# Layer norm row sums and squares on ScalarE instead of VectorE's batch norm passes, with some products moved from GpSimd to VectorE

## The chip, the cores and the metric

The kernel runs on one core of a Trainium2 chip. The metric is the device time of one execution in microseconds (us); lower is better. In a trace PE is TensorE, DVE is VectorE, ACT is ScalarE, POOL is GpSimd and SP is the engine that issues most of the DMAs.

## The reference

The input x has shape (2, 2048, 512). It goes through one block with modulation from a condition vector:

```python
h = layernorm(x) * (1 + ca) + sa
x = x + ga * mamba(h)          # in_proj, causal conv of 4 taps, silu, scan over 16 states, gate, out_proj
h = layernorm(x) * (1 + cb) + sb
x = x + gb * ffn(h)            # sum of 8 factor matrices, / sqrt(8), + bias
```

`layernorm(x)` is `(x - mean) / sqrt(var + 1e-5)` over the 512 features of a row. The heavy part is the scan inside `mamba`: for 1024 channels and 16 states, `s = s * exp(dt*A) + dt*h*B` along the sequence, and then the sum over the states of `s * C`. All data are fp32.

## The kernel before

The two sequences are cut into 16 chunks of 256 rows, taken in turn from the one and the other sequence (`CHUNKS` = 16, `ROWS` = 256, held as `LB` = 2 tiles of 128 rows). A chunk's scan is 64 units, a unit being one state index n for one pair of 128-channel tiles, 2 x 256 elements per partition. `one_round(c, ...)` exists once for each engine and runs 32 steps s of 2 units each; 4 units are a quad, so a chunk has 16 quads g. Every engine has its own fixed instruction order, and semaphores join them.

For each unit ACT computes the decays (two Exp passes, `decays`, L595) into one of three PSUM banks. DVE scans (`scan`, L1264). POOL makes the other scan input four units at a time (`make_ub`, L482, into a ring of `UB_RING` = 3). After the scan the state is multiplied by C, either by DVE (`multiply_c` of the vector block, L1277) or, for the last `POOLED[quad]` units of a quad, by POOL in one instruction for these units (`multiply_c` of the pool block, L520). PE turns the products and sums over n. ACT saves the last column of each state for the next chunk (`keep_carry`, L579), and a decay bank is free for the unit three places further on in the order `FREED` when the scan, or the product, of its unit is done.

Around this scan each round carries the neighbours' work: the first layer norm and projections of chunk c+1 (when `la` is given), and the output projection, the second layer norm and the ffn of chunk c-1 (when `lc` is given).

The statistics of a norm are made like this. DVE runs `bn_stats` on the two row tiles (`stats`, L1284; for the first norm in `stats_before(c + 2)` at s = 31, for the second in `stats_after(c - 1)` at s = 17) and `bn_aggr` (`means`, L1293) at s = 0 and at s = 18. POOL turns the variance into 1/sqrt(var + eps) (`deviations`, L447 and L449, called by `norm_before` at quad 0 and `norm_after` at quad 9, ahead of that quad's `make_ub`). DVE makes the shift, minus mean times that (`shifts`, L1300) at s = 1 and s = 19, between the two scans of the step. ACT normalizes (L602), at s = 3 in `z_before` and at s = 20 in `z_after`. In the second norm the row was finished just before by `residual_mixer` (L1365, L1367) at s = 15 and s = 17.

`scan(unit)` and `scan(unit + 1)` of a DVE step stand with this between them: the product of the unit before, then `means` or `shifts` where the step has them.

Of the kernel before, what the change touches and what calls it, by code (L numbers as in the profile page):

```python
# [22 lines left out]
ALU = mybir.AluOpType  # L23
ACT = mybir.ActivationFunctionType

P = 128
# [15 lines left out]
UB_RING = 3  # L42
# [4 lines left out]
DT_PAIRS = 5  # L47
ON_POOL = (2, 2, 2, 2, 3, 2, 3, 3, 3, 2, 2, 1, 2, 1, 1, 1)
FIRST_POOL = (2, 1, 1, 1, 1, 1, 2, 2, 2, 2, 2, 1, 2, 1, 1, 1)
LAST_POOL = (2, 2, 2, 2, 1, 2, 1, 2, 1, 2, 1, 2, 2, 2, 2, 1)  # L50
POOLED = FIRST_POOL + ON_POOL * (CHUNKS - 2) + LAST_POOL
EARLY = (46, 54)
# [92 lines left out]
def build(nc, x, win_m, xp_t, dt_t, wo_t, chan, cond_t, wmod, factors, bias, out):  # L145
# [9 lines left out]
    with ExitStack() as ctx:  # L155
# [42 lines left out]
        mv_a = sb("mv_a", [P, LB, 2])  # L198
        nrm_a = sb("nrm_a", [P, 2, LB])

        dt = sb("dt", [P, DT_PAIRS, 2, ROWS])
# [18 lines left out]
        mv_c = sb("mv_c", [P, LB, 2])  # L220
        nrm_c = sb("nrm_c", [P, 2, LB])

        mod_row = [hc[0:BATCH, 2 * j:2 * j + 2, :].rearrange("p k r -> p (k r)") for j in range(2)]
# [32 lines left out]

        xc_loaded, bn_c, stats_c, norm_c, z_c = sem("xc_loaded"), sem("bn_c"), sem("stats_c"), sem("norm_c"), sem("z_c")
        tanh_g_made, o_scaled, f_scaled, out_stored = sem("tanh_g_made"), sem("o_scaled"), sem("f_scaled"), sem("out_stored")

# [168 lines left out]
        def _(pool):  # L428
# [13 lines left out]

            def deviations(c, mv, nrm, done, normed, used):

                pool.wait_ge(done, c + 1)
                wait(pool, used, c)
                pool.tensor_tensor(nrm[:, 0, :], mv[:, :, 1], small[:, 1, :], ALU.add).then_inc(normed, 1)  # L447
                pool.wait_ge(normed, NORMS * c + 1)
                pool.tensor_tensor(nrm[:, 0, :], nrm[:, 0, :], small[:, 0, :], ALU.pow).then_inc(normed, 1)  # L449

            def norm_before(c):
                deviations(c, mv_a, nrm_a, stats_a, norm_a, z_a)

            def norm_after(c):
                deviations(c, mv_c, nrm_c, stats_c, norm_c, z_c)

# [78 lines left out]
            def one_round(c, par, la, lc):  # L535
                for g in range(QUADS):
                    quad = QUADS * c + g
                    if la is not None and g == 0:
                        norm_before(c + 1)
                    if lc is not None and g == 9:  # L540
                        norm_after(c - 1)
                    if quad + UB_RING - 1 < QUADS * CHUNKS:
                        make_ub(quad + UB_RING - 1)
                    multiply_c(quad)
                    if g in (0, 2, 3):
                        make_u(c, max(g, 1))
                    if c == 0 and 3 <= g < 3 + RANK - 1:
                        add_factor(g - 2)
                    if la is not None and g == 12:
                        make_u(c + 1, 0)  # L550

            rounds(one_round)
            for t in range(LB):
                pool.wait_ge(stats_c, FINAL + 1 + t)
                if t == 0:
                    pool.wait_ge(z_c, FINAL)
                pool.tensor_tensor(nrm_c[:, 0, t:t + 1], mv_c[:, t, 1:2], small[:, 1, 0:1], ALU.add).then_inc(norm_l, 1)
                pool.wait_ge(norm_l, 2 * t + 1)
                pool.tensor_tensor(nrm_c[:, 0, t:t + 1], nrm_c[:, 0, t:t + 1], small[:, 0, 0:1], ALU.pow).then_inc(norm_l, 1)
# [3 lines left out]
        def _(act):  # L563
# [42 lines left out]
            def modulate(src, dst, j, b, shift, scale):  # L606
# [5 lines left out]
                return last  # L612


            def z_before(c):
# [171 lines left out]
            def one_round(c, par, la, lc):  # L787
                for s in range(STEPS):
# [5 lines left out]
                    if la is not None:  # L794
# [9 lines left out]
                        if s in (23, 27):  # L804
                            soft_dt(c + 1, 2 * (s // 27))
                            soft_dt(c + 1, 2 * (s // 27) + 1)
                    if lc is not None and s == 22:
                        modulate_after(c - 1, 1 - par, 1)
# [20 lines left out]
                    if lc is not None:  # L829
                        if s in (1, 3, 5):  # L830
                            tanh_gate(c - 1, {1: 1, 3: 2, 5: 3}[s])
                        if s == 20:
                            z_after(c - 1)
                        if s == 21:
                            act.wait_ge(mods_made, 4)
                            modulate_after(c - 1, 1 - par, 0)
                    if la is not None and s == 29:
                        tanh_gate(c, 0)
                    if la is None and s in (20, 21, 23, 25):
                        tanh_gate_last({20: 0, 21: 1, 23: 2, 25: 3}[s])  # L840
# [405 lines left out]
        def _(dve):  # L1246
# [48 lines left out]

            def shifts(c, mv, nrm, normed):

                dve.wait_ge(normed, NORMS * c + 2)
                for t in range(LB):
                    dve.tensor_scalar(nrm[:, 1, t:t + 1], mv[:, t, 0:1], nrm[:, 0, t:t + 1], -1.0,  # L1300
                                      ALU.mult, ALU.mult).then_inc(normed, 1)
# [58 lines left out]
            def residual_mixer(c, par, t):  # L1360
# [5 lines left out]
                dve.wait_ge(o_scaled, LB * c + t + 1)  # L1366
                dve.tensor_tensor(xc[:, t, :], bank_c[t][:, :], xc[:, t, :], ALU.add).then_inc(c_free[t], 1)  # L1367

            def stats_after(c):
                dve.wait_ge(c_free[0], C_JOBS * c + 5)  # L1370
                dve.wait_ge(c_free[1], C_JOBS * c + 5)
                stats(c, xc, stat_c, bn_c, stats_c)

# [42 lines left out]
            means(0, stat_a, mv_a, bn_a, stats_a, norm_a)  # L1416
            shifts(0, mv_a, nrm_a, norm_a)
            copy_mod_rows(0)
# [19 lines left out]
            def one_round(c, par, la, lc):  # L1438
                for s in range(STEPS):
# [7 lines left out]
                    if la is not None and s == 0:  # L1447
                        means(c + 1, stat_a, mv_a, bn_a, stats_a, norm_a)
                    if la is not None and s == 1:
                        shifts(c + 1, mv_a, nrm_a, norm_a)  # L1450
                    if lc is not None and s == 18:
                        means(c - 1, stat_c, mv_c, bn_c, stats_c, norm_c)
                    if lc is not None and s == 19:
                        shifts(c - 1, mv_c, nrm_c, norm_c)
                    scan(unit + 1)
# [11 lines left out]
                    if lc is not None:  # L1467
# [6 lines left out]
                        if s in (15, 17):  # L1474
                            residual_mixer(c - 1, 1 - par, s // 17)
                        if s == 17:
                            stats_after(c - 1)
                        if s in (26, 27):
                            scale_ffn(c - 1, 1 - par, s - 26)
                    if la is not None:  # L1480
                        if s == 31 and c + 2 < CHUNKS:
                            stats_before(c + 2)
                        if s in (10, 12, 15, 17):
# [13 lines left out]
            for t in range(LB):  # L1497
# [6 lines left out]
                dve.wait_ge(c_free[t], c_jobs + 1)  # L1504
                if t == 0:
                    dve.wait_ge(stats_c, FINAL)
                dve.bn_stats(stat_c[:, t, :], xc[:, t, :]).then_inc(bn_c, 1)
                dve.wait_ge(bn_c, FINAL + 1 + t)
                if t == 0:
# [37 lines left out]
```

## Time and profile before

| what | value |
|---|---|
| median of 3 runs | 2100.62 us (2098.13 to 2101.44) |
| the profiled execution, its time | 2095.92 us |
| the profiled execution, its span | 2093.7 us |
| busy share of the span: DVE, POOL, PE, ACT | 93%, 91%, 81%, 71% |
| mean granted TensorE clock | 0.958 of full |

The span is the time from the first to the last instruction; 2.2 us of the profiled execution lie outside it. A duration in the trace is that of one instruction from its start to its end. Neighbours on one engine overlap a little, so the time that an instruction takes from its engine is the distance from its start to the start of the next.

### The profile page before, as it was taken

To read this page: it belongs to the slowest core of one execution; us is meant where nothing else is said; L and a number is where in the kernel's file an instruction comes from. 1 tells how busy PE (TensorE), PEld (TensorE's weight loads), DVE (VectorE), ACT (ScalarE), POOL (GpSimd) and SP (SyncE) were. 2 spreads that over 40 slices of the span, in tenths; PEclk is the share of its full clock that TensorE was granted. 3 is DMA by queue.
4 is the path that set the end of the run, shared out by engine and by line. 5 is a ranking of instruction groups with operands and counts; after the bars stand their busy time and mean duration, and the time that the engine had idled before them with its cause. 6 is when DMAs were issued, how large, how long until landed. Compare 5 with 4: busy or idle time off the path is not lost.

```text
span 2093.7 us, 28318 instructions
## 1 busy us (share of the span) xinstructions
PE 1694.9 (81%) x8640; PEld 1236.5 (59%) x8640; DVE 1949.5 (93%) x2473; ACT 1484.6 (71%) x4483; POOL 1905.3 (91%) x936
## 2 busy tenths in 40 slices
PE   7576787888878788888878888787887878788797
PEld 4365656656565665656556575655656565565564
DVE  3688999999999999999999999999999999999995
ACT  3456777687777777777677877767777776877662
POOL 0669999999999999999999999999999999999992
PEclk9778999999999999999999999999999999999998
DMA  6345404123040412304031131413213041310300
GB/s 241 136 101 106 136 21 151 41 92 96 26 151 22 151 41 86 96 32 145 28 136 56 72 106 36 142 31 132 61 52 125 21 152 36 118 60 33 109 26 31
DMA packets 70122, 179.80 MB, mean 86 GB/s; under 512 B 6609, under 2 KB 8273, under 8 KB 61906
## 3 DMA queue, kind: packets, MB, share of 16 engines
q1 hardware_dynamic: 66274, 170.65, 24.1%
q0 software_dynamic: 3696, 7.34, 2.2%
q8 instruction: 69, 1.13, 0.2%
q14 instruction: 83, 0.68, 0.1%
HBM read 169.05 MB, written 8.91 MB: 85 GB/s over the span
## 4 chain that ended last, share of the span: by engine, by line
DVE 49%; issue 19%; ACT 18%; PE 8%; DMA 3%; POOL 2%; DVEq 0%; ACTq 0%; SPq 0%; POOLq 0%
DVE state_p L1264 15%; DVE decay L1264 13%; DVE sc_d L1277 6%; ACT decay L595 6%; DVE bank_a L1317 6%; DMA ffn<-factors 2%; ACT dt L701 2%; DVE hc L1326 2%; ACT L595 2%; ACT L701 2%; DVE yg L1358 2%; PE bank_a L924 1%; PE y_bank L877 1%; DVE yg L1336 1%; POOL ub L482 1%
## 5 line engine op out<-in xcount | busy, mean ns | idle before, releaser
L482 POOL TENSOR_TENSOR ub<-u,b_all 128x2048 f32<-128x2048 f32 x255 | 1160.9, 4553 | 0.0
L595 ACT ACTIVATE decay<-dt,decay_rate 128x256 f32<-128x256 f32 (+1 forms) x2048 | 887.2, 465 | 168.0 <-DVE state_p L1264 165.5
L1264 DVE TENSOR_TENSOR_SCAN decay<-decay,carry,ub 128x512 f32<-128x512 f32 x526 | 656.2, 1273 | 37.3 <-ACT decay L595 16.1
L1264 DVE TENSOR_TENSOR_SCAN state_p<-decay,carry,ub 128x512 f32<-128x512 f32 x498 | 627.0, 1268 | 40.1 <-ACT decay L595 39.1
L520 POOL TENSOR_TENSOR state_p<-state_p,c_all 128x1024 f32<-128x1024 f32 (+2 forms) x256 | 587.9, 2297 | 54.6 <-ACT carry L579 50.6
L877 PE MATMUL y_bank<-ident,sc_d 128*128 128x128 f32 x2104 | 333.7, 290 | 238.5 <-DVE sc_d L1277 238.4
L877 PEld LDWEIGHTS y_bank<-ident,sc_d 128*128 128x128 f32 x2104 | 251.1, 148 | 330.8 <-DVE sc_d L1277 327.0
L1277 DVE TENSOR_TENSOR sc_d<-decay,c_all 128x512 f32<-128x512 f32 x526 | 348.9, 668 | 0.0
L877 PEld LDWEIGHTS y_bank<-ident,state_p 128*128 128x128 f32 x1992 | 236.2, 144 | 114.3 <-POOL state_p L520 71.9
L877 PE MATMUL y_bank<-ident,state_p 128*128 128x128 f32 x1992 | 272.1, 281 | 35.2 <-POOL state_p L520 33.6
L579 ACT ACTIVATE carry<-decay 128x2 f32<-128x2 f32 x526 | 85.6, 163 | 286.4 <-DVE sc_d L1277 286.3
L924 PE MATMUL bank_a<-hT,win_h 128*128 128x256 f32 x992 | 246.2, 393 | 2.3 <-ACT hT L610 2.3
L924 PE MATMUL bank_c<-hT,win_z 128*128 128x256 f32 x960 | 240.8, 399 | 0.0
L1006 PE MATMUL bank_c<-wo,yg 128*128 128x512 f32 x480 | 224.0, 595 | 0.0
L924 PEld LDWEIGHTS bank_c<-hT,win_z 128*128 128x128 f32 x960 | 187.9, 204 | 30.6 <-issue 6.7
L924 PEld LDWEIGHTS bank_a<-hT,win_h 128*128 128x128 f32 x992 | 185.3, 197 | 28.8 <-DVE hc L1326 5.0
L1317 DVE SCALAR_TENSOR_TENSOR bank_a<-pre_z,conv,bank_a 128x256 f32<-128x256 f32 x372 | 150.8, 478 | 11.8 <-ACT bank_a L647 11.8
L1006 PEld LDWEIGHTS bank_c<-wo,yg 128*128 128x128 f32 x480 | 89.1, 191 | 69.2 <-issue 65.6
L1030 PE MATMUL bank_c<-ffn,xa 128*128 128x512 f32 x240 | 123.6, 618 | 0.0
L461 POOL TENSOR_TENSOR u<-dt,hc 128x512 f32<-128x512 f32 x64 | 82.0, 1281 | 41.9 <-ACT dt L701 41.9
L868 PE MATMUL y_bank<-ident,skipped 128*128 128x128 f32 x256 | 41.3, 285 | 89.0 <-ACT y_rows L680 86.8
L680 ACT ACTIVATE y_rows<-y_bank 128x512 f32<-128x512 f32 x64 | 37.7, 589 | 71.6 <-PE y_bank L877 71.6
(135 smaller groups left out, 1765.0 us busy)
## 6 DMA issues: line engine op xcount, KB each, us to landing
win_h<-win_m SPq DMA_DIRECT2D x128, 256.0 KB, 2.6
c_all<-bc_scratch SPq DMA_DIRECT2D x32, 1024.0 KB, 7.4
win_z<-win_m SPq DMA_DIRECT2D x128, 256.0 KB, 2.7
b_all<-bc_scratch SPq DMA_DIRECT2D x31, 1024.0 KB, 4.9
xa<-x SPq DMA_DIRECT2D x16, 512.0 KB, 4.0
xc<-x SPq DMA_DIRECT2D x16, 512.0 KB, 3.7
out<-xc SPq DMA_DIRECT2D x15, 512.0 KB, 6.8
ffn<-factors POOLq DMA_DIRECT2D x7, 1024.0 KB, 9.2
```

The source lines that it names most:

```text
L482: pool.tensor_tensor(ub[:, slot, :, :, :], u[:, (PAIRS * c + q) % U_PAIRS, :, :].unsqueeze(1).to_broadcast([P, QUAD, 2, ROWS]), b_all[:, n ...
L520: pool.tensor_tensor(part, part, c_all[:, n + QUAD - k:n + QUAD, :].unsqueeze(2).to_broadcast([P, k, 2, ROWS]), ALU.mult).then_inc(pooled, 1)
L579: act.activation(dst, src, ACT.Copy).then_inc(carried, 1)
L595: last = act.activation(bk[:, j * ROWS + j:(j + 1) * ROWS], dt[:, pair % DT_PAIRS, j, j:], ACT.Exp, scale=decay_rate[:, e, n:n + 1])
L701: last = act.activation(dt[:, pair % DT_PAIRS, j, :], src, ACT.Softplus, bias=ch[:, e, DT_B:DT_B + 1])
L877: last = pe.matmul(y_bank[:, at:at + P], tile[:, j, t * P:(t + 1) * P], ident[:, :], start=False, stop=last_of_pair, is_transpose=True, sk ...
L924: last = pe.matmul(dst[:, j * ROWS:(j + 1) * ROWS], tile[:, k, :], hTc[:, k, :], start=(k == 0), stop=(k == KD - 1))
L1006: last = pe.matmul(bank_c[t][:, :], yg[:, k, t * P:(t + 1) * P], wo[:, k, :], start=(k == 0), stop=(k == KE - 1))
L1030: last = pe.matmul(bank_c[t][:, :], h2T[:, k, t * P:(t + 1) * P], ffn[:, k, :], start=False, stop=(k == KD - 1))
L1264: dve.tensor_tensor_scan(dst, bk[:, :], ub[:, quad % UB_RING, i, :, :].rearrange("p j r -> p (j r)"), carried_in[:, n, 2 * q:2 * q + 1], A ...
L1277: dve.tensor_tensor(sc_d[:, i % D_RING, :, :], bk[:, :].rearrange("p (j r) -> p j r", j=2), c_all[:, n:n + 1, :].to_broadcast([P, 2, ROWS] ...
L1317: dve.scalar_tensor_tensor(out=part, in0=pre[q % 2][:, j, k:k + ROWS], scalar=conv[:, e, k:k + 1], in1=part, op0=ALU.mult, op1=ALU.add).th ...
```

## The change

ACT takes over the sums. For the first norm of chunk c+2 it runs a Copy pass with an accumulated row sum over each row tile at s = 30 and 31 (`sum_before`), into a PSUM bank whose content nobody reads. DVE turns both sums into minus the mean over sqrt(512) in one `tensor_scalar` of 128x2 (`scaled_means`) at s = 0. ACT then runs two Square passes whose accumulated sum is the variance (`squares_before`) at s = 1. For the second norm the row sum comes out of the residual addition itself, which becomes a `scalar_tensor_tensor` with an accumulated output; DVE scales it at s = 18 (`means_after`) and ACT runs the two Square passes at s = 18 (`squares_after`), between the decays of units 37 and 38. `bn_stats` and `bn_aggr` go, except in the first two chunks' first norm and in the last chunk's second norm. On POOL the deviations of quad 0 and quad 9 move behind that quad's `make_ub`. The shifts of the first norm move from s = 1 to s = 2, those of the second norm move behind the second scan of s = 19. In the 14 middle chunks one product (quad 8) moves from POOL to DVE, and in every second of them (the odd ones) one more (quad 4).

```diff
-ON_POOL = (2, 2, 2, 2, 3, 2, 3, 3, 3, 2, 2, 1, 2, 1, 1, 1)
+ON_POOL = (2, 2, 2, 2, 3, 2, 3, 3, 2, 2, 2, 1, 2, 1, 1, 1)
+ODD_POOL = (2, 2, 2, 2, 2, 2, 3, 3, 2, 2, 2, 1, 2, 1, 1, 1)
-POOLED = FIRST_POOL + ON_POOL * (CHUNKS - 2) + LAST_POOL
+POOLED = FIRST_POOL + (ODD_POOL + ON_POOL) * (CHUNKS // 2 - 1) + LAST_POOL
...
             def norm_before(c):
-                deviations(c, mv_a, nrm_a, stats_a, norm_a, z_a)
+                if c < 2:
+                    pool.wait_ge(stats_a, c + 1)
+                else:
+                    pool.wait_ge(var_a, c - 1)
+                deviations(c, mv_a, nrm_a, norm_a, z_a)
             def norm_after(c):
-                deviations(c, mv_c, nrm_c, stats_c, norm_c, z_c)
+                pool.wait_ge(var_c, c + 1)
+                deviations(c, mv_c, nrm_c, norm_c, z_c)
...
                     quad = QUADS * c + g
+                    if quad + UB_RING - 1 < QUADS * CHUNKS:
+                        make_ub(quad + UB_RING - 1)
                     if la is not None and g == 0:
                         norm_before(c + 1)
                     if lc is not None and g == 9:
                         norm_after(c - 1)
-                    if quad + UB_RING - 1 < QUADS * CHUNKS:
-                        make_ub(quad + UB_RING - 1)
                     multiply_c(quad)
...
+            def sum_before(c, t):
+                if t == 0:
+                    act.wait_ge(xa_loaded, 16 * c + 16)
+                    act.wait_ge(dt_made, PAIRS * c)
+                    wait(act, mean_a, c - 2)
+                act.activation(bank_a[t][:, :], xa[:, t, :], ACT.Copy, accum_out=sum_a[:, t:t + 1]).then_inc(sums_a, 1)
+            def squares(c, src, mv, junk, done):
+                for t in range(LB):
+                    last = act.activation(junk[t][:, :], src[:, t, :], ACT.Square, bias=mv[:, t, 0:1],
+                                          scale=DIM ** -0.5, accum_out=mv[:, t, 1:2])
+                last.then_inc(done, 1)
+            def squares_before(c):
+                act.wait_ge(mean_a, c - 1)
+                squares(c, xa, mv_a, bank_a, var_a)
+            def squares_after(c):
+                act.wait_ge(mean_c, c + 1)
+                squares(c, xc, mv_c, bank_c, var_c)
...
+                    if la is not None and c and s == 1:
+                        squares_before(c + 1)
...
                     decays(2 * step + 1)
...
+                        if s == 18:
+                            squares_after(c - 1)
...
+                    if c + 2 < CHUNKS and s in (30, 31):
+                        sum_before(c + 2, s - 30)
...
+            def scaled_means(c, sums, mv, normed, made):
+                dve.wait_ge(normed, NORMS * c)
+                dve.tensor_scalar(mv[:, :, 0], sums[:, :], -DIM ** -1.5, None, ALU.mult).then_inc(made, 1)
...
-                dve.tensor_tensor(xc[:, t, :], bank_c[t][:, :], xc[:, t, :], ALU.add).then_inc(c_free[t], 1)
-            def stats_after(c):
-                dve.wait_ge(c_free[0], C_JOBS * c + 5)
-                dve.wait_ge(c_free[1], C_JOBS * c + 5)
-                stats(c, xc, stat_c, bn_c, stats_c)
+                if t == 0:
+                    wait(dve, mean_c, c)
+                dve.scalar_tensor_tensor(out=xc[:, t, :], in0=bank_c[t][:, :], scalar=1.0, in1=xc[:, t, :], op0=ALU.mult,
+                                         op1=ALU.add, accum_out=sum_c[:, t:t + 1]).then_inc(c_free[t], 1)
...
                     if la is not None and s == 0:
-                        means(c + 1, stat_a, mv_a, bn_a, stats_a, norm_a)
-                    if la is not None and s == 1:
-                        shifts(c + 1, mv_a, nrm_a, norm_a)
+                        means_before(c + 1)
+                    if la is not None and s == 2:
+                        shifts(c + 1, mv_a, nrm_a, norm_a, DIM ** 0.5 if c else -1.0)
                     if lc is not None and s == 18:
-                        means(c - 1, stat_c, mv_c, bn_c, stats_c, norm_c)
-                    if lc is not None and s == 19:
-                        shifts(c - 1, mv_c, nrm_c, norm_c)
+                        means_after(c - 1)
                     scan(unit + 1)
...
-                        if s == 17:
-                            stats_after(c - 1)
+                        if s == 19:
+                            shifts(c - 1, mv_c, nrm_c, norm_c, DIM ** 0.5)
...
-                        if s == 31 and c + 2 < CHUNKS:
-                            stats_before(c + 2)
```

## Rows read from the trace of the kernel before

**Rows 1.** The page, busy time and share of each engine.
```profile
PE 1694.9 (81%) x8640; PEld 1236.5 (59%) x8640; DVE 1949.5 (93%) x2473; ACT 1484.6 (71%) x4483; POOL 1905.3 (91%) x936
```

**Rows 2.** Tile nrm_a, 200 to 2000 us: durations, first and last start.
```profile
L447 POOL TENSOR_TENSOR nrm_a<-mv_a,small x14: 194/194/197, 225.7 to 1826.4; 128x2 f32<-128x2 f32 x14
```

**Rows 3.** Who waited for whom, 228 to 1829 us, on DVE and POOL: total, times, longest.
```profile
DVE state_p L1264 <- ACT decay L595: 26.9, 28, 1.8
...
POOL nrm_a L447 <- DVE mv_a L1293: 19.8, 13, 1.5
POOL state_p L520 <- ACT carry L579: 9.3, 15, 0.7
```

**Rows 4.** DVE by line and shape: busy us, mean ns, idle before.
```profile
L1277 DVE TENSOR_TENSOR sc_d<-decay,c_all 128x512 f32<-128x512 f32 x526 | 348.9, 668 | 0.0
...
L1300 DVE TENSOR_SCALAR nrm_a<-mv_a,nrm_a 128x1 f32<-128x1 f32 x32 | 5.2, 203 | 4.4 <-POOL nrm_a L449 4.4
...
L1425 DVE TENSOR_SCALAR decay_rate<-decay_rate 128x128 f32<-128x128 f32 x1 | 0.2, 221 | 0.0
L1414 DVE TENSOR_SCALAR conv<-ch 128x40 f32<-128x40 f32 x1 | 0.2, 176 | 0.0
```

**Rows 5.** POOL by line and shape.
```profile
L520 POOL TENSOR_TENSOR state_p<-state_p,c_all 128x1024 f32<-128x1024 f32 x130 | 306.3, 2356 | 12.0 <-ACT carry L579 8.0 <-DVE decay L1264 2.0 <-issue 0.4
L520 POOL TENSOR_TENSOR state_p<-state_p,c_all 128x1536 f32<-128x1536 f32 x56 | 192.5, 3438 | 0.0
```

**Rows 6.** ACT by line and shape.
```profile
L639 ACT ACTIVATE pre_z<-bank_a 128x512 f32<-128x512 f32 x62 | 35.9, 580 | 0.0
...
L602 ACT ACTIVATE xa<-xa,nrm_a 128x512 f32<-128x512 f32 x32 | 24.1, 800 | 5.1 <-DVE nrm_a L1300 5.1
```

**Rows 7.** DVE in order of time around a chunk's start: start, us.
```profile
1084.64 0.66 DVE L1277 TENSOR_TENSOR sc_d<-decay,c_all 128x512 f32<-128x512 f32 x1
1085.22 1.28 DVE L1284 BATCH_NORM_STATS2 stat_a<-xa 128x6 f32<-128x512 f32 x2
1086.41 1.27 DVE L1264 TENSOR_TENSOR_SCAN decay<-decay,carry,ub 128x512 f32<-128x512 f32 x1
1087.60 0.22 DVE L1293 BATCH_NORM_AGGREGATE mv_a<-stat_a 128x2 f32<-128x6 f32 x2
1087.74 1.26 DVE L1264 TENSOR_TENSOR_SCAN decay<-decay,carry,ub 128x512 f32<-128x512 f32 x1
```

**Rows 8.** POOL in order of time around the same chunk's start.
```profile
1085.10 1.28 POOL L520 TENSOR_TENSOR state_p<-state_p,c_all 128x512 f32<-128x512 f32 x1 [0.66 <-ACT carry L579]
...
1088.82 4.53 POOL L482 TENSOR_TENSOR ub<-u,b_all 128x2048 f32<-128x2048 f32 x1
```

**Rows 9.** DVE in order of time, two tensor_scalar operations of 512 elements.
```profile
77.97 4.00 DVE L1404 TENSOR_SCALAR ga<-ga 128x512 f32<-128x512 f32 x1
...
101.87 0.43 DVE L1404 TENSOR_SCALAR gb<-gb 128x512 f32<-128x512 f32 x1
```

**Rows 10.** POOL in order of time, beside the first of these.
```profile
76.75 4.94 POOL L482 TENSOR_TENSOR ub<-u,b_all 128x2048 f32<-128x2048 f32 x1
```

**Rows 11.** DVE in order of time, s = 17 to 19 of the same chunk.
```profile
1155.29 0.69 DVE L1367 TENSOR_TENSOR xc<-bank_c,xc 128x512 f32<-128x512 f32 x1
...
1157.27 0.67 DVE L1326 SCALAR_TENSOR_TENSOR hc<-tanh_s,bank_a 128x512 f32<-128x512 f32 x1
...
1159.05 0.22 DVE L1293 BATCH_NORM_AGGREGATE mv_c<-stat_c 128x2 f32<-128x6 f32 x2
1159.19 1.26 DVE L1264 TENSOR_TENSOR_SCAN decay<-decay,carry,ub 128x512 f32<-128x512 f32 x1
...
1160.95 1.27 DVE L1264 TENSOR_TENSOR_SCAN state_p<-decay,carry,ub 128x512 f32<-128x512 f32 x1
```

**Rows 12.** POOL in order of time, quad 8 of the same chunk.
```profile
1157.58 3.43 POOL L520 TENSOR_TENSOR state_p<-state_p,c_all 128x1536 f32<-128x1536 f32 x1
```

**Rows 13.** ACT in order of time, after the decays of unit 38.
```profile
1161.07 0.17 ACT L579 ACTIVATE carry<-decay 128x2 f32<-128x2 f32 x1 [3.27 <-DVE sc_d L1277]
```

More of the change, by code:

```diff
@@ L199, in build @@
         nrm_a = sb("nrm_a", [P, 2, LB])
+        sum_a = sb("sum_a", [P, LB])
         dt = sb("dt", [P, DT_PAIRS, 2, ROWS])
@@ L221, in build @@
         nrm_c = sb("nrm_c", [P, 2, LB])
+        sum_c = sb("sum_c", [P, LB])
         mod_row = [hc[0:BATCH, 2 * j:2 * j + 2, :].rearrange("p k r -> p (k r)") for j in range(2)]
@@ L257, in build @@
         xc_loaded, bn_c, stats_c, norm_c, z_c = sem("xc_loaded"), sem("bn_c"), sem("stats_c"), sem("norm_c"), sem("z_c")
+        sums_a, mean_a, var_a, mean_c, var_c = sem("sums_a"), sem("mean_a"), sem("var_a"), sem("mean_c"), sem("var_c")
         tanh_g_made, o_scaled, f_scaled, out_stored = sem("tanh_g_made"), sem("o_scaled"), sem("f_scaled"), sem("out_stored")
@@ L441, in _, with deviations @@
             pool.wait_ge(ident_set, 2)
-            def deviations(c, mv, nrm, done, normed, used):
-                pool.wait_ge(done, c + 1)
+            def deviations(c, mv, nrm, normed, used):
                 wait(pool, used, c)
@@ L553, in _ @@
             for t in range(LB):
-                pool.wait_ge(stats_c, FINAL + 1 + t)
+                pool.wait_ge(stats_c, 1 + t)
                 if t == 0:
@@ L1294, in means, with means_before, means_after, shifts @@
                 last.then_inc(done, 1)
-            def shifts(c, mv, nrm, normed):
+            def scaled_means(c, sums, mv, normed, made):
+                dve.wait_ge(normed, NORMS * c)
+                dve.tensor_scalar(mv[:, :, 0], sums[:, :], -DIM ** -1.5, None, ALU.mult).then_inc(made, 1)
+            def means_before(c):
+                if c < 2:
+                    means(c, stat_a, mv_a, bn_a, stats_a, norm_a)
+                else:
+                    dve.wait_ge(sums_a, LB * (c - 1))
+                    scaled_means(c, sum_a, mv_a, norm_a, mean_a)
+            def means_after(c):
+                for t in range(LB):
+                    dve.wait_ge(c_free[t], C_JOBS * c + 5)
+                if c:
+                    scaled_means(c, sum_c, mv_c, norm_c, mean_c)
+                else:
+                    dve.tensor_scalar(mv_c[:, :, 0], sum_c[:, :], -DIM ** -1.5, None, ALU.mult).then_inc(mean_c, 1)
+            def shifts(c, mv, nrm, normed, factor):
                 dve.wait_ge(normed, NORMS * c + 2)
                 for t in range(LB):
-                    dve.tensor_scalar(nrm[:, 1, t:t + 1], mv[:, t, 0:1], nrm[:, 0, t:t + 1], -1.0,
+                    dve.tensor_scalar(nrm[:, 1, t:t + 1], mv[:, t, 0:1], nrm[:, 0, t:t + 1], factor,
                                       ALU.mult, ALU.mult).then_inc(normed, 1)
@@ L1416, in _ @@
             means(0, stat_a, mv_a, bn_a, stats_a, norm_a)
-            shifts(0, mv_a, nrm_a, norm_a)
+            shifts(0, mv_a, nrm_a, norm_a, -1.0)
             copy_mod_rows(0)
@@ L1504, in _ @@
                 dve.wait_ge(c_free[t], c_jobs + 1)
-                if t == 0:
-                    dve.wait_ge(stats_c, FINAL)
                 dve.bn_stats(stat_c[:, t, :], xc[:, t, :]).then_inc(bn_c, 1)
-                dve.wait_ge(bn_c, FINAL + 1 + t)
+                dve.wait_ge(bn_c, 1 + t)
                 if t == 0:
```

## The prediction

> **What bounds the kernel now.** I read the busy shares of the page first. DVE and POOL are both over 90% busy, ACT has 29% of the span free [rows 1]. The norm of one chunk comes 123.1 us after that of the last: 14 of them lie from 225.7 to 1826.4 us, 13 distances [rows 2]. So the 14 middle chunks carry 1,723 us of the span, and each microsecond per chunk is worth about 14. The waits over 13 of these chunks are few [rows 3]. DVE waits 26.9 us for decays of ACT (its largest wait), 2.1 per chunk. POOL waits in two places only: 19.8 us for DVE's mean (1.52 at each chunk's start) and 9.3 us for a carry at quad 15. So both engines stand close to the limit, DVE a little closer, and whatever stops either of them in mid-chunk is paid nearly in full.
>
> **What DVE loses and gains.** An instruction's price is the distance between starts. Two `bn_stats` take 1.19 us, from 1085.22 to 1086.41, and two `bn_aggr` take 0.14 us, from 1087.60 to 1087.74 [rows 7]. A chunk has two of each pair: 2.66 us go. Added are 21 products over 14 chunks, 1.5 per chunk, at 0.58 us (1084.64 to 1085.22 [rows 7]), which is 0.87 us. The two `tensor_scalar` of 128x2 are not in the trace. They lie between a `bn_aggr`'s distance of 0.07 and the 0.20 of the 128x1 form [rows 4]; I take 0.1 each. The accumulated output of the two additions isn't in the trace either. It costs from nothing to another small instruction, 0.2; I take 0.1 each. That is 1.27 us added, so DVE is shorter by 1.39 us per chunk (1.1 to 1.6), 19.5 us over 14 chunks.
>
> **What POOL gains.** One product is 3438 - 2356 = 1,082 ns of a POOL instruction [rows 5], so 1.6 us per chunk, and its 1.52 us of waiting for the mean has work in front of it now. POOL is the looser of the two afterwards, so this covers DVE's gain and adds nothing to it.
>
> **What ACT gets.** Six passes of 128x512 per chunk, between 580 ns (no pointer operand) and 800 ns (two) [rows 6]. I take 0.65 us of ACT's time each and 0.1 for the accumulated sum (0 to 0.2), so 4.5 us, plus 1.5 more carries and seams. ACT is free for 29% of 123 us, some 35 us, so the amount is covered. The Copy passes at s = 30 and 31 fall where it waits for DVE. The place of one pair is not covered. `squares_after` stands between the decays of units 37 and 38 and waits for `mean_c`, which DVE makes at s = 18 just before scan 37. From there DVE has 1.76 us of work until scan 38 (1159.19 to 1160.95 [rows 11]). ACT needs about 0.1 to start, 1.5 for two squares, and 0.1 and 0.87 for carry and decays: 2.6 us. Before, these decays were long made, since ACT then sat 3.27 us [rows 13]. So DVE waits 0.8 us at each second norm (0.3 to 1.2 with the bounds of the passes), 12 us over 15 chunks. At s = 1 the same pair stands before the decays of unit 3, which need DVE's product of unit 0 anyway, so it is hidden. If Square needed a function table of its own, there would be four loads more per chunk on ACT; I expect none.
>
> **The new step that matters: two elements on DVE while POOL works.** The trace shows what a `tensor_scalar` with an immediate, from SBUF to SBUF, does beside POOL [rows 9, 10]. One of 512 elements takes 0.43 us in one case and 4.00 us in another. In the long case it began at 77.97, POOL's product had run since 76.75 and ended at 81.69, and the DVE operation ended at 81.97. It stood still until POOL's instruction was over. Undisturbed it needs 0.43 us for elements for which `tensor_tensor` needs 0.67 [rows 4], so it runs at a doubled rate. Small ones do too: from 40 to 128 elements the time grows by 45 ns, 0.51 ns per element [rows 4]. The 128x1 form shows no such stop, its mean is 203 ns though POOL was at work beside nearly all of them [rows 4]. The new form with two elements lies between them. I hold it for one that stops, since it is the doubled form with one element for each half.
>
> The Trainium skill (VectorE: DVE Perf Modes, Mode 2×_2P) states that this mode needs one source and the destination in SBUF and an even outermost dimension. By that two elements run in it and one doesn't; no row here shows a two-element form. By the row of the 128x1 form the sum below would be 2093 us, by the rule it stays as it is.
>
> Where do the two land? Take the second norm first. `means_after` came at 1159.05 [rows 11]. In the new order DVE is there earlier by 1.24 us (one `bn_stats` pair, `bn_aggr` less the new one) and by 1.28 (the 1.98 us from 1155.29 to 1157.27 become 0.7), and later by 0.1 (the first accumulated output) and 0.58 (the moved product of quad 8): 1157.2, and 1157.8 in odd chunks, which move one more. POOL's product of quad 8 began at 1157.58 [rows 12]. POOL starts its chunk's first `make_ub` at 1086.34 in place of 1088.82 [rows 8] and does the 0.9 us of the norm behind it, so it is 1.6 us earlier: 1156.0, until 1158.3 with two units. In even chunks DVE waits 1.1 us for it. In odd chunks POOL is 1.08 us earlier still: it ended at 1157.3, and the next `make_ub` of 4.55 us has begun, to 1161.8. DVE waits 4.0 us. Seven of each are 35.7 us (0 to 4.6 each is the bound).
>
> At the chunk's start it is a near tie. Without `bn_stats` scan 0 starts at 1085.22, and the new operation is due 1.19 us on, at 1086.41 [rows 7]. POOL's product of quad 15 ends at 1085.10 + 1.28 = 1086.38, and `make_ub` follows it at once now, since the norm no longer stands in front of it [rows 8]. If POOL is first, DVE stops for 4.53 us, less some hundredths; if DVE is first, for nothing. The starts speak for POOL by 0.07 us. But a POOL instruction needs some time from its start to its first read, and in the one case at hand DVE got in between two of POOL's instructions [rows 9, 10]. I take DVE as first, at a little better than even.
>
> **The sum.** -19.5 + 12 + 35.7 = +28.2 us. The deviations behind `make_ub` at quad 9 come 0 to 1 us late for DVE's shifts of s = 19, in chunks where DVE has not just waited; I take nothing, since the wait for ACT covers it. Against its own time the profiled execution goes from 2095.92 to 2124.1. The median of the runs is 4.7 us above the profiled one, so 2129 us.
>
> **Rivals.**
> 1. POOL is first at the chunk's start, in most chunks. The Trainium skill (SBUF — State Buffer, Who interferes with whom) says that whoever issues first holds the shared pair for its whole instruction; the trace agrees, 3.7 us of waiting in [rows 9, 10]. The price: 14 x 4.45 = 62 us more, less what DVE then finds done: 2129 + 60 = 2189 us. Half of the chunks give 2160. For it speaks the order of the starts, against it that 0.03 us of a shorter scan decides. Chance 0.28.
> 2. The small operation does not stop, as the 128x1 form doesn't. Only the gain, the wait for the squares and a late shift remain: -19.5 + 12 + 0 to 5 us, 2093 to 2098. Chance 0.14.
> 3. The clean gain, the other side: nothing stops DVE, and the squares are done in time because ACT's passes cost the lower bound. It decides when two squares with their sums take under 0.8 us or the decays of unit 38 are still done in time: -19.5 (to -22) us, 2081 us (2078 to 2085). For it speaks ACT's 3.27 us of rest at this place [rows 13], against it the order of ACT's instructions. Chance 0.22.
>
> **Chances and range.** The forecast (stops at s = 18, none or few at s = 0) has 0.36; its own range is 2108 to 2150, from the bounds of the passes and of the 35.7 us. Within 0.2% (4.2 us, about what runs of this kernel can tell) falls the upper part of rival 2. Faster: 0.22 and part of 0.14, together 0.28. Same: 0.08. Slower: 0.36 + 0.28, 0.64. The range must take in rivals 1 and 3 to leave out no more than 2 in 10: 2077 to 2188.
>
> **What would show each step.** The idle time of POOL before L447 is gone. The new `tensor_scalar` is short (0.1 to 0.2 us) where POOL is idle or between instructions, and 1 to 4.6 us long where POOL works; its longest ends stand just behind the end of a POOL instruction. DVE waits for the decays of unit 38 by 0.8 us at each second norm. The distance of chunks is 123.1 + 2 = 125 us; at 127 or more rival 1 holds, at 121.7 rival 3. The prediction is wrong if the two-element form doesn't take the second port, if POOL's phase at quad 8 is another than worked out (half a microsecond there moves 4.5 us per chunk), or if the tie goes to POOL.

## The result

The changed kernel takes 2202.74 us (median of 4 runs, 2200.18 to 2203.27) against 2099.38 us for the kernel before: 1.049 times its time, 95% interval 1.047 to 1.051. The forecast was 2129 us with a range to 2188 us. The direction was right and the size was not: 103 us came, 28 were forecast, and the time lies above the range.

### The profile page after: what moved, and what is told of

The parts are those of the page before. It is cut to its first block and busy times, and to the rows that moved or that the text cites. A ratio compares the mean times of both kernels' runs of the same rounds, so it can differ in the third digit from the quotient of the medians.

```text
span 2200.9 us, 28516 instructions
## 1 busy us (share of the span) xinstructions
PE 1735.6 (79%) x8640; PEld 1275.7 (58%) x8640; DVE 1983.8 (90%) x2437; ACT 1551.1 (70%) x4697; POOL 1884.2 (86%) x936
## 5 line engine op out<-in xcount | busy, mean ns | idle before, releaser
L603 ACT ACTIVATE decay<-dt,decay_rate 128x256 f32<-128x256 f32 (+1 forms) x2048 | 887.0, 465 | 130.5 <-DVE state_p L1301 128.2
L528 POOL TENSOR_TENSOR state_p<-state_p,c_all 128x1024 f32<-128x1024 f32 (+2 forms) x256 | 565.4, 2209 | 183.5 <-ACT carry L587 183.0
L1301 DVE TENSOR_TENSOR_SCAN decay<-decay,carry,ub 128x512 f32<-128x512 f32 x547 | 682.7, 1275 | 38.4 <-ACT decay L603 16.3
L1301 DVE TENSOR_TENSOR_SCAN state_p<-decay,carry,ub 128x512 f32<-128x512 f32 x477 | 602.8, 1270 | 47.6 <-ACT decay L603 46.4
L914 PE MATMUL y_bank<-ident,sc_d 128*128 128x128 f32 x2188 | 353.9, 297 | 207.7 <-DVE sc_d L1314 207.3
L914 PEld LDWEIGHTS y_bank<-ident,sc_d 128*128 128x128 f32 x2188 | 273.4, 153 | 296.6 <-DVE sc_d L1314 290.4
L1314 DVE TENSOR_TENSOR sc_d<-decay,c_all 128x512 f32<-128x512 f32 x547 | 363.2, 668 | 0.0
L914 PE MATMUL y_bank<-ident,state_p 128*128 128x128 f32 x1908 | 267.2, 284 | 33.2 <-POOL state_p L528 31.9
L961 PE MATMUL bank_c<-hT,win_z 128*128 128x256 f32 x960 | 248.3, 408 | 0.0
L905 PE MATMUL y_bank<-ident,skipped 128*128 128x128 f32 x256 | 47.4, 316 | 135.9 <-ACT y_rows L711 133.8
L905 PEld LDWEIGHTS y_bank<-ident,skipped 128*128 128x128 f32 x256 | 31.4, 159 | 150.1 <-issue 147.2
```

What stands on the lines that cost most here:

```text
L528: pool.tensor_tensor(part, part, c_all[:, n + QUAD - k:n + QUAD, :].unsqueeze(2).to_broadcast([P, k, 2, ROWS]), ALU.mult).then_inc(pooled, 1)
L603: last = act.activation(bk[:, j * ROWS + j:(j + 1) * ROWS], dt[:, pair % DT_PAIRS, j, j:], ACT.Exp, scale=decay_rate[:, e, n:n + 1])
L914: last = pe.matmul(y_bank[:, at:at + P], tile[:, j, t * P:(t + 1) * P], ident[:, :], start=False, stop=last_of_pair, is_transpose=True, sk ...
L961: last = pe.matmul(dst[:, j * ROWS:(j + 1) * ROWS], tile[:, k, :], hTc[:, k, :], start=(k == 0), stop=(k == KD - 1))
L1301: dve.tensor_tensor_scan(dst, bk[:, :], ub[:, quad % UB_RING, i, :, :].rearrange("p j r -> p (j r)"), carried_in[:, n, 2 * q:2 * q + 1], A ...
L1314: dve.tensor_tensor(sc_d[:, i % D_RING, :, :], bk[:, :].rearrange("p (j r) -> p j r", j=2), c_all[:, n:n + 1, :].to_broadcast([P, 2, ROWS] ...
```

## The profile after

The span is 2200.9 us. Its busy shares, in the order of the page:

```profile
PE 1735.6 (79%) x8640; PEld 1275.7 (58%) x8640; DVE 1983.8 (90%) x2437; ACT 1551.1 (70%) x4697; POOL 1884.2 (86%) x936
```

Both bounding engines lost share against [rows 1]: 3 points on DVE, 5 on POOL. DVE's busy time even grew, by 34 us, though it has fewer passes. So part of its busy time is standing still, and POOL now waits. The norm's place in each chunk (tile nrm_a, 200 to 2000 us, durations and first and last start):

```profile
L450 POOL TENSOR_TENSOR nrm_a<-mv_a,small x14: 196/196/198, 232.0 to 1928.0; 128x2 f32<-128x2 f32 x14
```

That is 130.5 us per chunk in place of 123.1 [rows 2]. DVE's two new operations, tiles mv_a and mv_c (durations minimum, median, maximum in ns):

```profile
L1336 DVE TENSOR_SCALAR mv_a<-sum_a x14: 708/4466/4497, 225.1 to 1921.9; 128x2 f32<-128x2 f32 x14
...
L1336 DVE TENSOR_SCALAR mv_c<-sum_c x14: 156/158/1408, 428.1 to 2114.8; 128x2 f32<-128x2 f32 x14
```

The same operation on 128x2 takes 4.47 us at the chunk's start and 0.16 us at s = 18. The waits from 228 to 1829 us, the stretch of [rows 3], which holds 12 of these longer chunks (total us, times, longest), DVE and then POOL:

```profile
DVE nrm_c L1357 <- POOL nrm_c L452: 52.6, 12, 4.6
DVE state_p L1301 <- ACT decay L603: 30.2, 24, 1.8
...
POOL state_p L528 <- ACT carry L587: 121.8, 65, 4.0
POOL nrm_a L450 <- ACT bank_a L634: 16.4, 12, 1.4
```

The first line is new: 4.4 us each time for the deviation of the second norm. POOL waits 121.8 us for carries in place of 9.3 [rows 3]: in part because it is ahead while DVE stands, in part, 2.6 to 4.0 us per chunk, at quad 8 for the reason told below. The 16.4 us before the first norm's deviation were 19.8 us before the change; they are now a wait for the squares.

In order of time, the start of one chunk, DVE and then POOL (start, us). It answers to [rows 7, 8]:

```profile
1136.51 1.28 DVE L1301 TENSOR_TENSOR_SCAN decay<-decay,carry,ub 128x512 f32<-128x512 f32 x1
1137.70 4.46 DVE L1336 TENSOR_SCALAR mv_a<-sum_a 128x2 f32<-128x2 f32 x1
1142.08 1.28 DVE L1301 TENSOR_TENSOR_SCAN decay<-decay,carry,ub 128x512 f32<-128x512 f32 x1
```

```profile
1136.39 1.28 POOL L528 TENSOR_TENSOR state_p<-state_p,c_all 128x512 f32<-128x512 f32 x1 [0.67 <-ACT carry L587]
1137.62 4.52 POOL L490 TENSOR_TENSOR ub<-u,b_all 128x2048 f32<-128x2048 f32 x1
```

`make_ub` began 0.08 us ahead of the operation, ended at 1142.14, and the operation ended at 1142.16. DVE lost 1142.08 - 1137.70 = 4.38 us, less the 0.1 that the operation needs by itself. Here are steps 17 to 19 of the chunk before, on DVE, POOL and ACT. They answer to [rows 11 to 13]:

```profile
1078.04 1.27 DVE L1301 TENSOR_TENSOR_SCAN state_p<-decay,carry,ub 128x512 f32<-128x512 f32 x1
...
1082.35 0.16 DVE L1336 TENSOR_SCALAR mv_c<-sum_c 128x2 f32<-128x2 f32 x1
...
1084.95 1.28 DVE L1301 TENSOR_TENSOR_SCAN state_p<-decay,carry,ub 128x512 f32<-128x512 f32 x1 [0.69 <-ACT decay L603]
...
1092.37 0.33 DVE L1357 TENSOR_SCALAR nrm_c<-mv_c,nrm_c 128x1 f32<-128x1 f32 x2 [4.36 <-POOL nrm_c L452]
```

```profile
1084.30 2.35 POOL L528 TENSOR_TENSOR state_p<-state_p,c_all 128x1024 f32<-128x1024 f32 x1 [3.94 <-ACT carry L587]
1086.62 4.52 POOL L490 TENSOR_TENSOR ub<-u,b_all 128x2048 f32<-128x2048 f32 x1
...
1091.64 0.69 POOL L452 TENSOR_TENSOR nrm_c<-nrm_c,small 128x2 f32<-128x2 f32 x1
```

```profile
1082.54 0.69 ACT L634 ACTIVATE bank_c<-xc,mv_c 128x512 f32<-128x512 f32 x1 [1.38 <-DVE mv_c L1336]
...
1083.87 0.19 ACT L634 ACTIVATION_READ_ACCUMULATOR bank_c<-xc,mv_c 128x1 f32 x1
1083.97 0.19 ACT L587 ACTIVATE carry<-state_p 128x4 f32<-128x4 f32 x1
```

Read them from the bottom up. The carry of POOL's units of quad 8 could be taken when their last scan ended (1079.31), but in ACT's order it stands behind the squares, and these wait for DVE's mean (1082.35 plus its 0.16). So POOL's product starts at 1084.30, after 3.94 us of waiting. `make_ub` begins at 1086.62, and the deviation stands behind it until 1092.33. DVE wanted it at 1088.0.

Per chunk this is 4.38 - 0.1 at the start, 4.36 at step 19, and 0.5 more of waiting for decays (0.69 at unit 38, where DVE had not waited before, less 0.17 that it had waited for them some units later), less the forecast gain of 1.4: 7.7 us. Measured are 130.5 - 123.1 = 7.4 as a mean over 13 distances. Over the whole span, DVE by line and shape (busy us, mean ns, idle before):

```profile
L1336 DVE TENSOR_SCALAR mv_a<-sum_a 128x2 f32<-128x2 f32 x14 | 58.9, 4204 | 0.0
...
L1357 DVE TENSOR_SCALAR nrm_c<-mv_c,nrm_c 128x1 f32<-128x1 f32 x30 | 5.0, 209 | 62.9 <-POOL nrm_c L452 62.9
...
L1426 DVE DVE_READ_ACCUMULATOR xc<-bank_c,xc 128x1 f32 x30 | 2.5, 83 | 0.0
```

## The experiments

Lines are cut to their core. Each kernel is the changed one with the edit named, unless said otherwise. Ratios are to the kernel before, run on the same chip; its median was 2096.28 us beside the first four experiments, 2096.75 and 2099.9 us beside later ones, so kernels measured on different chips are compared by their distance from it. The changed kernel was 103 us above it.

**Each two-element operation as two of one element.**

```diff
-dve.tensor_scalar(mv[:, :, 0], sums[:, :], -DIM ** -1.5, None, ALU.mult).then_inc(made, 1)
+for t in range(LB):
+    last = dve.tensor_scalar(mv[:, t, 0:1], sums[:, t:t + 1], -DIM ** -1.5, None, ALU.mult)
+last.then_inc(made, 1)
```

> The changed kernel with each 128x2 tensor_scalar of the scaled means split into two of 128x1, nothing else. Theory (the two-element form takes the port that POOL holds, the one-element form doesn't): the 14 stops of 4.4 us at the chunk's start go, and the wait for the second norm's deviation stays at 4.3 us per chunk, since POOL still waits there for a carry behind the squares: 14 x 4.4 = 61 us less, 2141 us. Rival (the operation really waits for something else at that point, ScalarE's sums or the semaphores): the first of the two takes 4 us and more, and the time stays at 2203 us. Second rival (POOL's lead over DVE comes from the stop, and without it the second wait shrinks too): 2085 to 2120 us.

Measured: 2145.96 us, 1.024 (1.022 to 1.025), 50 us above the kernel before. Its operations and its largest wait:

```profile
L1337 DVE TENSOR_SCALAR mv_a<-sum_a x28: 142/147/152, 222.8 to 1867.7; 128x1 f32<-128x1 f32 x28
...
DVE nrm_c L1361 <- POOL nrm_c L452: 56.8, 13, 4.5
```

In order of time at one chunk's start, POOL and then DVE:

```profile
1109.21 4.54 POOL L490 TENSOR_TENSOR ub<-u,b_all 128x2048 f32<-128x2048 f32 x1
...
1109.28 0.19 DVE L1337 TENSOR_SCALAR mv_a<-sum_a 128x1 f32<-128x1 f32 x2
```

All 28 take 0.15 us at the place where one of two elements took 4.47, and `make_ub` has begun 0.07 us ahead of them as it had there. The data and the place are the same, so it is the form: two elements stop beside a working POOL, one doesn't. (The two lie a step of two apart in `mv_a`; a dense pair wasn't tried, but the dense 512 elements of [rows 9] stopped too.) The wait at step 19 is untouched, so it has a cause of its own and doesn't hang on the stop.

**The second norm's deviation in front of `make_ub` at quad 9 again**, as it stood before the change.

```diff
+                    if lc is not None and g == 9:
+                        norm_after(c - 1)
                     if quad + UB_RING - 1 < QUADS * CHUNKS:
                         make_ub(quad + UB_RING - 1)
...
-                    if lc is not None and g == 9:
-                        norm_after(c - 1)
```

> The changed kernel with norm_after of quad 9 back in front of that quad's make_ub on POOL, nothing else. Theory (DVE's shifts of step 19 wait because the deviation stands behind a make_ub of 4.5 us that begins late): the deviation is done 0.4 us before DVE wants it, the wait of 4.3 us goes, 14 x 4.4 = 61 us less, 2141 us; the stop of 4.4 us at the chunk's start stays. Rival (the wait comes from ScalarE's squares being late, whatever POOL's order): the wait stays over 3 us, 2190 us or more. Second rival (the make_ub that is now 0.9 us later makes DVE wait for its scan input): 2150 us or more, with waits of DVE for ub.

Measured: 2099.22 us, 1.001 (1.000 to 1.002). Nearly all of the loss was gone: 3 us above the kernel before in place of 103, so 100 us where the theory said 61. The wait at step 19 went as expected, though POOL still waits 3.96 us for the late carry at quad 8 (2.6 to 4.0 us in each chunk):

```profile
1036.87 2.35 POOL L528 TENSOR_TENSOR state_p<-state_p,c_all 128x1024 f32<-128x1024 f32 x1 [3.96 <-ACT carry L587]
...
1040.50 0.31 DVE L1357 TENSOR_SCALAR nrm_c<-mv_c,nrm_c 128x1 f32<-128x1 f32 x2
```

That the stop at the chunk's start shrank too, from 4.47 to 0.43 us with the two-element form in place, was in no expectation:

```profile
L1336 DVE TENSOR_SCALAR mv_a<-sum_a x14: 409/428/667, 224.9 to 1823.8; 128x2 f32<-128x2 f32 x14
```

Its POOL, at one chunk's start; the two-element operation ran from 1086.48, for 0.42 us:

```profile
1085.61 1.27 POOL L528 TENSOR_TENSOR state_p<-state_p,c_all 128x512 f32<-128x512 f32 x1
1086.84 4.53 POOL L490 TENSOR_TENSOR ub<-u,b_all 128x2048 f32<-128x2048 f32 x1
```

In the changed kernel this product of quad 15 had waited 0.67 us for its carry, and in the kernel before 0.66 us [rows 8]. A POOL that waits there is released by DVE's own progress, and its `make_ub` then begins 0.06 to 0.08 us ahead of DVE's operation. It is so at every chunk's start with this wait, in every kernel traced here that has the operation at this place. Now there is no such wait. DVE no longer gives POOL 4.4 us in mid-chunk, so POOL reaches quad 15 later, DVE's operation comes 0.4 us before that product ends, and goes in between. So the stop at the chunk's start hung on the wait at step 19: a wait of DVE puts POOL ahead, and a POOL that is ahead has just begun a `make_ub` when DVE's operation comes. The reverse doesn't hold, as the run with one-element operations showed.

**Both edits.**

> Both edits: two 128x1 operations in place of each 128x2 one, and the second norm's deviation in front of make_ub. Theory (two separate stops that add): 2203 - 61 - 61 = 2081 us, so under the kernel before (2099 us) by 0.9%. Rival (the two stops cover one work of POOL's, and taking both away shows POOL as the bound): 2100 us or more.

Measured: 2100.76 us, 1.002 (1.001 to 1.003), where the theory said 2081. The two gains don't add, since moving the deviation already takes most of the stop with it. The trace has one more thing. DVE waits 1.9 to 3.6 us for decays in four chunks, three early and one late, 10.9 us in all, behind an ACT that waits 4.03 us for TensorE in the first of them. TensorE's matmuls took twice as long just before, and the granted clock was near half (us, then busy time and number of PE, PEld, DVE, ACT, POOL, granted clock, DMA):

```profile
437.00:443.00 6.00, 6.00 (x19) 3.24 (x18) 4.19 (x5) 4.65 (x14) 5.97 (x2) 0.58 0.00 1
443.00:452.00 9.00, 8.22 (x42) 5.20 (x39) 5.42 (x7) 4.77 (x15) 7.11 (x5) 1.00 0.32 117
```

Of 2.4 GHz this is near the lower level of 1.2, after TensorE had waited 1.95 us for a product of POOL's at 431.5. In the other two early chunks it was 0.56 and 0.57, in the late one 0.66, and 1.00 in seven chunks without such a wait. Why it fell in these four wasn't tried. They bear out the coupling: at the chunk's start that follows each of the four, `make_ub` begins 0.08 us ahead of DVE's operation, and in the middle chunks without such a wait POOL is still in its product of quad 15 there.

**The operation of the first norm in front of scan 0**, 1.2 us earlier.

```diff
+                    if la is not None and s == 0 and c:
+                        means_before(c + 1)
                     scan(unit)
...
-                    if la is not None and s == 0:
+                    if la is not None and s == 0 and not c:
                         means_before(c + 1)
```

> The changed kernel with the 128x2 operation of the first norm in front of scan 0 of its chunk instead of behind it, so that it arrives 1.2 us earlier. Theory (it stops until whichever POOL instruction runs at its arrival is over): it now meets POOL's product of quad 15 (1.28 us) and is done just behind its end, 1.2 to 1.4 us after its start instead of 4.5: 14 x 3.1 = 43 us less, 2160 us. Rival (the stop always lasts for a make_ub, because POOL's next instruction gets in first): 4.5 us and more as before, 2203 us or more. Rival (it waits for ScalarE's sum): it would end at the same moment as before the edit, 2203 us.

Measured: 2157.27 us, 1.029 (1.027 to 1.031), 61 us above the kernel before in place of 103: 42 us less, where the first theory said 43. The operation:

```profile
L1336 DVE TENSOR_SCALAR mv_a<-sum_a x14: 1177/1182/1509, 223.0 to 1879.5; 128x2 f32<-128x2 f32 x14
```

The stop lasts for the rest of the POOL instruction that is running, here the 1.28 us product. POOL's next one doesn't get in first. With the wait at step 19 in place (52.6 us, as in the changed kernel) this edit saves only the stop.

**The squares of the second norm behind the decays of unit 38.**

```diff
-                        if s == 18:
-                            squares_after(c - 1)
...
+                    if lc is not None and s == 19:
+                        squares_after(c - 1)
                     decays(2 * step + 1)
```

> The changed kernel with the squares of the second norm one place later on ScalarE, behind the decays of unit 38, nothing else. Theory (POOL's product of quad 8 starts 4 us late because the carry of unit 35 stands in ScalarE's order behind the squares, which wait for DVE's mean; the late make_ub then holds the deviation and DVE's shifts): that product starts at once, DVE's wait of 4.4 us for the deviation shrinks to about 1.1 us, and its wait of 0.7 us for the decays of unit 38 goes; the stop at the chunk's start may stay: 14 x 4.0 = 56 us less, 2147 us; if the stop goes too, as it did when the deviation was moved, 2090 us. Rival (only the place of the deviation behind make_ub matters): the wait stays over 4 us, 2190 us or more.

Measured: 2163.86 us, 1.032 (1.031 to 1.034), 67 us above the kernel before: 36 us less than the changed kernel, not 56. The carry is free and POOL's product starts early, but the two-element operation of s = 18 then meets it:

```profile
L1336 DVE TENSOR_SCALAR mv_c<-sum_c x14: 816/1466/1569, 425.0 to 2079.7; 128x2 f32<-128x2 f32 x14
...
DVE nrm_c L1357 <- POOL nrm_c L452: 11.6, 12, 1.2
```

Per chunk 4.36 + 0.69 us went and 1.38 + 0.97 came, 2.7 us, 38 us in all. The stop at the chunk's start stayed at 4.46 us. This is the stop at s = 18 that the prediction had described; in the changed kernel the late carry had kept POOL away from it.

**The same with one-element operations.**

> The changed kernel with one-element scaled means and the squares behind the decays of unit 38; the deviation stays behind make_ub. Theory (with the squares moved, what DVE loses at steps 18 and 19 is one make_ub that ends too late, 1.4 us of it at the two-element operation and 1.0 us at the shifts, and without the two-element form all 2.3 us stand at the shifts; at the chunk's start 4.4 us go): 2164 - 14 x 4.4 = 2103 us, with 2 to 2.5 us of waiting for the deviation in each chunk. Rival (the 1.4 us were DVE's own and go as well): 2083 us.

Measured: 2110.01 us, 1.005 (1.003 to 1.006), 7 us over the first theory's time. The wait at the shifts over 13 chunks:

```profile
DVE nrm_c L1361 <- POOL nrm_c L452: 29.6, 13, 2.5
```

That is 2.3 us each: the 1.4 us moved there, as the theory said. What sets DVE's time past this place is the end of one `make_ub`; without the stop DVE only comes to it earlier and waits longer. It also parts the 4.36 us of the changed kernel: 2.3 us come from the deviation's place behind `make_ub` alone, the other 2 from the late carry.

**Three edits: one-element operations, deviation first, squares later.**

> Three edits: one-element scaled means, deviation of the second norm in front of make_ub, squares behind the decays of unit 38. Theory (what was left over the arithmetic gain was 0.7 us per chunk of DVE waiting for decays behind the squares, 0.3 us of the two-element operation and 0.5 us near step 27): 122.3 us per chunk go to 121.7, some 10 us under the kernel with the first two edits, 2088 us, 0.4% under the kernel before. Rival (DVE then catches up with ScalarE at the table loads of steps 23 and 27 and waits there): 2097 us, no gain over the kernel before.

Measured: 2074.85 us, 0.989 (0.988 to 0.991). Better than the theory by 13 us; the theory started from the kernel with two edits, whose four long waits for decays (10.9 us, at the lower clock) are gone here. 121.6 us per chunk are left. This kernel has the whole change without its stops and late shifts, and is 22 us faster than the kernel before.

**The three edits and the products as before the change.**

```diff
-ON_POOL = (2, 2, 2, 2, 3, 2, 3, 3, 2, 2, 2, 1, 2, 1, 1, 1)
+ON_POOL = (2, 2, 2, 2, 3, 2, 3, 3, 3, 2, 2, 1, 2, 1, 1, 1)
-POOLED = FIRST_POOL + (ODD_POOL + ON_POOL) * (CHUNKS // 2 - 1) + LAST_POOL
+POOLED = FIRST_POOL + ON_POOL * (CHUNKS - 2) + LAST_POOL
```

> The same three edits and the products as in the kernel before (1.5 per chunk back from DVE to POOL). Theory (DVE is the bound, at 0.58 us per product): 0.9 us per chunk less, 12 us under the kernel with the three edits, 2076 us. Rival (POOL, at 1.08 us per product, is the bound once DVE has lost its norm passes): 2088 to 2110 us, with DVE waiting for ub.

Measured: 2061.42 us, 0.983 (0.982 to 0.984), the fastest of all. Its chunk takes 120.6 us, and POOL's waits are down to this over 13 chunks:

```profile
POOL state_p L528 <- ACT carry L587: 1.2, 1, 1.2
POOL state_p L528 <- issue: 0.4, 2, 0.2
```

**The kernel before with the new split of the products alone.**

> The kernel before with the new split of the products alone, statistics untouched. Theory (DVE bound): 21 products x 0.58 us = +12 us, 2108 us, 0.6% slower. Rival (POOL bound before): up to 10 us faster. Rival (balanced, each has slack for it): within 4 us of the kernel before.

Measured: 2110.02 us, 1.006 (1.005 to 1.008), 13 us slower. Together with the run before (13 us between the two splits) this prices the moved products: DVE pays for them in either kernel, and what POOL is spared doesn't shorten the time.

**The fastest kernel with the two-element operations back.**

> The fastest kernel so far (2061 us: one-element scaled means, deviation in front of make_ub, squares behind the decays of unit 38, products as in the kernel before) with the two-element operations put back, all else kept. Theory (the form stops for the rest of whatever POOL runs): in that kernel's trace the operation at the chunk's start falls 0.4 us before the end of POOL's product of quad 15, which costs 0.3 us per chunk, 4 us in all; the one at step 18 falls 0.07 us behind the start of POOL's product of quad 8 of 3.4 us, which may cost up to 3.4 us per chunk more: between 2065 and 2112 us, the largest stops ending just behind an end of POOL's. Rival (the form is harmless once the other two places are mended): 2061 us.

Measured: 2160.49 us, 1.028 (1.027 to 1.030), 61 us above the kernel before where the same kernel with one-element operations was 35 below it, and 48 us over the upper end of the theory:

```profile
L1336 DVE TENSOR_SCALAR mv_a<-sum_a x14: 421/4496/4503, 225.4 to 1887.6; 128x2 f32<-128x2 f32 x14
...
L1336 DVE TENSOR_SCALAR mv_c<-sum_c x14: 1390/3120/3354, 417.9 to 2079.0; 128x2 f32<-128x2 f32 x14
```

The theory read the phases off a trace without stops, and had the one at s = 18 right (3.1 us in the median). That stop puts POOL ahead, and the next chunk's start then costs 4.5 us. The order of events shows it: the operation at 347.5 us took 0.42 us, the first long stop at s = 18 came at 417.9, and every chunk's start from 473.6 us on stopped for 4.5. It is the same one-way coupling, set off this time by the operation itself.

## Why the prediction was wrong

- **What bounds the kernel**: right. DVE bounds it more than POOL; 21 products cost 13.3 us, 0.63 us each where 0.58 were taken. (POOL had three places where it waited, not two: 1.8 us for DVE's scans was left out, which changes nothing.)
- **What DVE loses and gains**: right in size. The kernel with the three edits is 21.9 us faster than the one before, where this term said 19.5. ACT's squares were right too: 0.72 us each with the read of the sum (0.69 us and its 0.19 overlap a little), 0.75 taken. The accumulated output of DVE is an instruction of 0.083 us that the next one overlaps wholly: 0.62 us from the addition's start to the next, where another `scalar_tensor_tensor` of this size takes 0.59 or 0.60 (0.1 was taken), the 128x2 form undisturbed takes 0.16 us and 0.05 of distance.
- **Two elements on DVE while POOL works**: right. By the rule of the Trainium skill (VectorE: DVE Perf Modes, Mode 2×_2P) both ports are used when source and destination lie in SBUF and the outermost dimension that isn't one is even, or odd and equal in both. The prediction left out the odd case, without effect here: two elements meet the rule, one leaves no such dimension. The runs agree, 4.47 us against 0.15 at the same place.
- **The near tie at the chunk's start**: wrong side. POOL was first by 0.08 us, which is the 0.07 that was read from the starts, and it was set aside for an argument about its first read. This is rival 1, with 13 stops of 4.4 us. The prediction's argument left out what decides it: where POOL waits for the carry of quad 15, it is just ahead each time, and where it doesn't, DVE comes while the product still runs and stops for 0.43 us.
- **The stop at s = 18, 35.7 us forecast**: wrong step. The phase of POOL was worked out from its own chain alone. That its product of quad 8 waits for a carry that stands behind the squares in ACT's order was not followed, though these squares were seen to wait for DVE's mean. POOL came 2.6 to 4.0 us later than its own work asked, so DVE's operation met nothing (0.16 us). With the squares moved away the stop was there, 1.47 us in every chunk.
- **The deviation behind `make_ub`, "0 to 1 us late", taken as nothing**: the term of the sum that failed most. It was 4.36 us per chunk, 63 us in all. About half of it is the late carry, the rest the place behind `make_ub`: with an early carry 2.3 us stayed, and with the deviation in front all of it went, late carry or not. The reason given for nothing, that the wait for ACT covers it, failed too: DVE waited 0.69 us for the decays of unit 38 (0.8 were forecast), and still 4.36 us for the deviation.
- **The sum**: 19.5 us of gain stand against 57 us of the tie (58.9 less 14 x 0.16), 63 of the deviation and 7 for the decays of unit 38 (0.5 per chunk): +107.5 us, and the two spans differ by 107.2 (the medians by 103). That it closes so well is partly luck, since the gain in it is the forecast one. The range ended 1 us short of rival 1's own 2189 us and had no case with both.

What the terms don't show is that they were coupled in one direction, from a wait in mid-chunk to the stop at the next chunk's start; the run with the deviation moved back showed it, and the last run confirmed it. Left open: why TensorE's clock fell in four chunks of one kernel.

## What to carry to other kernels

When an instruction that waits is put into an engine's order, go through everything behind it until the next instruction that the engine would have waited for anyway, the few-element copies too: a carry of 0.19 us behind two squares and a deviation of 0.9 us behind a `make_ub` led to 63 us of waiting here. On DVE beside a busy POOL, give a small `tensor_scalar` one element per partition, or accept that its price is whatever POOL has left of its instruction. And where two engines run neck and neck, a wait of one shifts where the other is when they next meet, so price stops together, not one by one.

## What the runs showed of the hardware

- A `tensor_scalar` of 128x2 from SBUF to SBUF takes 0.16 us alone and up to 4.5 us beside a POOL `tensor_tensor`, ending 0.02 or 0.03 us behind that one's end; those of 128x1 take 0.14 to 0.16 us each, with POOL in a product, in a `make_ub` or idle.
- With starts 0.08 us apart the earlier one went first: 13 of the 14 operations at a chunk's start stopped for 4.4 us or more. A DVE operation that already waits when a POOL instruction ends goes ahead of POOL's next one, which costs that one nothing that can be seen: in the kernel with the deviation moved back these `make_ub` took 4.53 us, the others 4.54.
- Square with a bias operand and an accumulated sum, 128x512 from SBUF to PSUM: 0.68 us and 0.19 us for the read of the sum; two of them with their reads take 1.43 us from the first start to the next instruction. The Copy without operands takes 0.58 us. Neither brought a table load: there are 63 in both kernels.
